# Windowed attention and a 3x3 convolution on one core: one pair of operand stacks instead of two, the work of a unit reordered with a lead per stage, and the row maxima sent through memory

## The reference, cut to what matters

```python
def attention(x):                      # x: (2, 128, 128, 128), already group-normed
    g = clip((x * ac_w + ac_b) * x, 0.0, 6.0)
    q, k, v = windows_and_heads(einsum('bchw,dc->bdhw', g, qkv_w))    # (3, windows, 16, 64, 8)
    attn = softmax(einsum('wnqd,wnkd->wnqk', q, k) * 8 ** -0.5)
    o = einsum('wnqk,wnkd->wnqd', attn, v)
    return einsum('bchw,dc->bdhw', o, proj_w) + proj_b

x = x + attention(group_norm(x))
x = x + conv3x3(group_norm(x), W) + bias
```

## Time and profile before

| | |
|---|---|
| Median of 3 runs | 1791.33 us (1789.05 to 1791.84) |
| Time of the profiled execution | 1795.36 us |
| Its span in the trace | 1793.6 us |
| Busy share of the span: PE, DVE, ACT, POOL | 66%, 55%, 46%, 32% |
| Mean granted clock of TensorE | 0.757 of full |
| DMA, mean over the span | 107 GB/s |

### The profile page before, as it was taken

How to read it: one execution, slowest core, us unless ns; L and a number is a source line. 1 busy time by engine, 2 the same in 40 slices (tenths; PEclk the granted TensorE clock), 3 DMA queues, 4 the chain that set the end, 5 groups by cost and what they waited for, 6 DMA issues and landing times. The chain is left out here.

```text
span 1793.6 us, 62241 instructions
## 1 busy us (share of the span) xinstructions
PE 1177.2 (66%) x25315; PEld 686.1 (38%) x25315; DVE 990.1 (55%) x1379; ACT 824.8 (46%) x1231; POOL 578.0 (32%) x502
## 2 busy tenths in 40 slices
PE   1466666676567767587747665675766667657886
PEld 0244434444344444233314443443444444433332
DVE  7544444444454542699965543544444444418998
ACT  1345545455445553444424554454554555434443
POOL 4122322223222222466521232222231322225665
PEclk8568777777777775699965876776786777658999
DMA  5454544444454550022336453444453544400111
GB/s 207 118 134 126 136 114 115 110 125 125 121 119 114 133 134 22 1 94 100 106 115 161 133 132 103 121 113 107 123 133 97 132 116 127 110 2 12 58 47 71
DMA packets 169202, 191.30 MB, mean 107 GB/s; under 512 B 30208, under 2 KB 145280, under 8 KB 167936
## 3 DMA queue, kind: packets, MB, share of 16 engines
q1 hardware_dynamic: 168960, 187.58, 38.8%
HBM read 118.29 MB, written 67.11 MB: 103 GB/s over the span
## 5 line engine op out<-in xcount | busy, mean ns | idle before, releaser
L485 ACT ACTIVATE work<-ps,ws 128x1024 f32<-128x1024 f32 x256 | 283.9, 1109 | 319.4 <-PE ps L915 317.8
L693 DVE TENSOR_REDUCE m_all<-ps 128x16 f32<-128x1024 f32 x256 | 311.7, 1218 | 133.9 <-PE ps L899 133.7
L940 PE MATMUL ps<-work,v_ext 128*32 128x64 f32 x8192 | 216.1, 261 | 206.5 <-ACT work L485 202.1
L401 POOL TENSOR_TENSOR g_lo<-work,g_hi 128x512 f16<-128x512 f32 x64 | 74.4, 1162 | 673.8 <-ACT g_hi L525 673.8
L940 PEld LDWEIGHTS ps<-work,v_ext 128*32 128x32 f32 x8192 | 166.4, 134 | 248.1 <-issue 125.0
L395 POOL TENSOR_SCALAR work<-work 128x256 f32<-128x256 f32 x128 | 108.5, 848 | 349.5 <-DVE work L687 349.5
L948 PE MATMUL ps<-work,adds 128*32 128x128 f32 x4096 | 210.8, 334 | 0.0
L861 PE MATMUL ps<-work,c_hi 128*128 128x512 f16 x384 | 151.0, 393 | 68.3 <-DVE work L781 68.2
L719 DVE BATCH_NORM_STATS2 st<-img (+1 forms) x64 | 44.4, 694 | 252.7 <-POOL img L408 252.7
L572 ACT CAST work<-work 128x640 f16<-128x640 f32 x128 | 91.7, 718 | 144.4 <-DVE work L777 97.5
L781 DVE TENSOR_TENSOR work<-work 128x640 f16<-128x640 f32 x128 | 152.9, 1197 | 5.0 <-ACT work L572 4.6
(11 more groups left out here) (125 smaller groups left out, 2020.5 us busy)
## 6 DMA issues: line engine op xcount, KB each, us to landing
stack_scratch<-work SPq DMA_DIRECT2D x128, 256.0 KB, 2.2
k_bd<-stack_scratch SPq DMA_DIRECT2D x256, 96.0 KB
q_pl<-stack_scratch SPq DMA_DIRECT2D x128, 192.0 KB, 3.6
q_bd<-stack_scratch SPq DMA_DIRECT2D x256, 96.0 KB
k_pl<-stack_scratch SPq DMA_DIRECT2D x128, 192.0 KB, 4.9
stack_scratch<-work SPq DMA_DIRECT2D x128, 128.0 KB, 2.1
out_dram<-work SPq DMA_DIRECT2D x32, 512.0 KB, 2.7
img<-in_x_dram SPq DMA_DIRECT2D x8, 1024.0 KB, 13.8
```

The costliest lines, as they stand in the source:

```text
L485: a.activation(probs[:, p % 2, :], ps[:, ST_B:ST_B + 2, :].rearrange("p w t -> p (w t)"), ACT.Exp, scale=ws[:, R_EXP:R_EXP + 1]).then_inc( ...
L693: v.tensor_reduce(m_all[:, 0, :, p], ps[:, S_B:S_B + 2, :].rearrange("p r (a k) -> p (r a) k", k=WIN), AX.X, ALU.max).then_inc(max_done, 1)
L940: t_.matmul(ps[32 * k:32 * k + 32, PV_B + p // 2, at:at + WIN], v_pair(md, 2 * p + w, k)[:, 2 * HD * j:2 * HD * j + VC], probs[:, p % 2, c ...
```

## The change

It does five things, all in the attention stage.

1. One pair of stacks. `k_bd` and `q_pl` go. The first scores use `q_bd` and `k_pl` too, now with three buffers each; q is the stationary side, 64 columns at a time, so `scores(p)` is 32 matmuls of 64 columns instead of 16 of 128. Per unit 6 loads of 768 KB in all go.
2. Another order, in which each step names its unit by a lead, from 4 units ahead to 4 behind, and 40 iterations instead of 38. The statistics are taken 4 units late.
3. The hardware loop has 3 iterations in its body and 8 turns, so 7 jumps back for each batch.
4. The affine step is made by VectorE instead of ScalarE.
5. The maxima are written to memory (`max_scratch`, one DMA), and once this has landed two DMAs read them into `q_bd`. The write waits for the loads of the unit before, and the loads and writes of q and k stand behind this wait in SP's queue.

The diff, cut to its core (the reordered calls are those of the lists above, with their waits):

```diff
-TWO = 2
-TURN = 6
+FIRST = 4
...
+    maxd = nc.dram_tensor("max_scratch", [BUFS, PAIRS * HEADS, 2, P], F16, kind="Internal").ap()
...
-        q_pl = sb("q_pl", [P, TWO, HG, UT], F16)
-        k_bd = sb("k_bd", [P, TWO, HG, HJ, UT], F16)
-        k_pl = sb("k_pl", [P, TWO, HG, UT], F16)
-        q_bd = sb("q_bd", [P, TWO, HG, HJ, UT], F16)
+        k_pl = sb("k_pl", [P, BUFS, HG, UT], F16)
+        q_bd = sb("q_bd", [P, BUFS, HG, HJ, UT], F16)
...
+            for i in range(-FIRST, FIRST):
...
+                one(i, i % BUFS, live_at(i))
+            with eng.Fori(0, (UNITS - 2 * FIRST) // BUFS) as t:
+                for k in range(BUFS):
+                    one(t * BUFS + (FIRST + k), (FIRST + k) % BUFS, live_at(FIRST))
+            for i in range(UNITS - FIRST, UNITS + FIRST):
+                one(i, i % BUFS, live_at(i))
...
+                    if live(1):
+                        mb = (m + 1) % BUFS
+                        after(sp, m_hi_done, n + 1)
+                        after(sp, m_lo_done, n + 1)
+                        after(sp, m_in, n)
+                        sp.dma_start(maxd[mb], m_pair[:, :, :]).then_inc(m_sent, 16)
+                        after(sp, m_sent, n + 1)
+                        after(sp, st_done, n + 1 - BUFS)
                         for r in range(HR):
...
+                            at = 64 * r + ROWS
+                            sp.dma_start(q_bd[at:at + 2, mb, :, :, :].rearrange("s g j (p t) -> s (g j) p t", p=PAIRS),
+                                         maxd[mb, 32 * r:32 * r + 32].rearrange("(a p) s t -> s a p t", p=PAIRS)).then_inc(m_in, 16)
+                    if live(3):
+                        after(sp, q_in, n + 2)
+                        after(sp, k_in, n + 2)
+                        write(0, q_lo_done, q_hi_done, q_sent)
+                        write(1, k_lo_done, k_hi_done, k_sent)
+                        after(sp, st_done, n + 3 - BUFS)
+                        after(sp, q_sent, n + 3)
...
+                        after(sp, k_sent, n + 3)
...
+                        after(dve, gpre_done, n + 3)
+                        v.tensor_scalar(aff.rearrange("p (r c) -> p r c", r=WS), img[:, bass.ds(row, WS), bass.ds(col, UCOL)],
+                                        cf[:, A_SLOPE:A_SLOPE + 1], cf[:, A_OFF:A_OFF + 1], ALU.mult, ALU.add).then_inc(aff_done, 1)
...
-                    def scores(p):
-
-                        after(pe, max_done, n + 1, p)
+                    def scores(d, md, p):
+
+                        after(pe, max_done, d, p)
                         settle(pe)
                         for g in range(HG):
...
+                            for j in range(HJ):
+                                for w in range(2):
+                                    tok = slice((2 * p + w) * WIN, (2 * p + w + 1) * WIN)
+                                    at = g * P + j * WIN
+                                    for r in range(HR):
+                                        rows = slice(64 * r, 64 * r + ROWS)
+                                        mm = t_.matmul(ps[64 * w:64 * w + 64, S_B + r, at:at + WIN],
+                                                       q_bd[rows, md, g, j, tok], k_pl[rows, md, g, tok],
+                                                       start=True, stop=True)
```

More of the change, by code:

```diff
@@ L192, in build, with iterations, live_at @@
         block = ctx.enter_context(nc.Block())
[L194 to L202, removed]
-                    late()
[L204 to L209, removed]
+        def iterations(eng, b, one, late=None, at=1 - FIRST):
+            def live_at(i):
+                return lambda lead: 0 <= i + lead < UNITS
+            for i in range(-FIRST, FIRST):
+                if i == at and late:
+                    late()
+                one(i, i % BUFS, live_at(i))
[4 more added lines that the diff above has]
+                one(i, i % BUFS, live_at(i))
         def conv_units(eng, b, one):
@@ L286, in spread @@
                                 at = 64 * r + HROWS * j
[L287 to L291, removed]
-                        for r in range(HR):
[L293 to L315, removed]
+                                sp.dma_start(q_bd[at:at + HROWS, m, :, j, :], q_rows[r, j]).then_inc(q_in, 16)
+                        after(sp, k_sent, n + 3)
+                        k_rows = stackd[m, 1].rearrange("(r g a) s t -> r (a s) g t", r=HR, g=HG)
+                        for r in range(HR):
+                            sp.dma_start(k_pl[64 * r:64 * r + ROWS, m, :, :], k_rows[r]).then_inc(k_in, 16)
                 iterations(sp, b, one)
@@ new lines, in one @@
+                    if live(-4):
+                        row, col = pixels(i - 4)
+                        after(dve, x1_done, n - 4)
+                        v.bn_stats(st[:, bass.ds(i - 4, 1), :].rearrange("p a s -> p (a s)"),
+                                   img[:, bass.ds(row, WS), bass.ds(col, UCOL)]).then_inc(bn_done, 1)
+                    if live(1):
+                        row_max(n + 1, 2)
+                    if live(-1):
+                        scale(n - 1, 1)
+                    if live(1):
+                        row_max(n + 1, 3)
@@ L951, in weigh @@
                         mm.then_inc(pv_done, 1)
-                    def output(d):
-                        after(pe, o_done, d)
-                        t_.matmul(ps[:, GB, :], pw[:, :], o_n, start=True, stop=True).then_inc(proj_done, 1)
-                    me = (m - 1) % TURN
-                    if "B" in on:
-                        after(pe, g_lo_done, n + 2)
-                        after(pe, res_done, n - 3)
-                        if "R" not in on:
-                            after(pe, k_lo_done, n + 1)
-                        if peeled(i, -2) and b:
+                    if live(-1):
+                        weigh(n - 1, (m - 1) % BUFS, 3)
@@ new lines, in one @@
+                    if live(0):
+                        after(pe, m_in, n)
+                        scores_t(n, m, 0)
+                    if live(1):
+                        scores(n + 1, (m + 1) % BUFS, 2)
+                    if live(2):
+                        after(pe, q_lo_done, n + 2)
+                        v_rows()
+                    if live(3):
+                        after(pe, g_lo_done, n + 3)
+                        if live(-2):
+                            after(pe, res_done, n - 2)
+                        else:
+                            after(pe, k_lo_done, n + 2)
+                        if peeled(i, -3) and b:
@@ L1005, in one @@
-                    if "C" in on:
-                        after(pe, scaled_out, n - 1)
-                        after(pe, near_out, n - 1)
+                    if live(0):
+                        scores_t(n, m, 1)
+                    if live(1):
+                        scores(n + 1, (m + 1) % BUFS, 3)
+                    if live(0):
+                        weigh(n, m, 0)
+                    if live(3):
+                        after(pe, v_out, n + 2)
+                        project(0, GA, q_done)
@@ L1008, in one @@
+                    if live(1):
+                        if live(-1):
+                            after(pe, scaled_out, n - 1)
+                            after(pe, near_out, n - 1)
+                        else:
+                            after(pe, m_lo_done, n)
                         after(pe, max_done, n + 1)
```

272 lines of the change are left out of this document (110 added, 162 removed).

## The result

The changed kernel takes 1514.06 us (median of 4 runs, 1509.85 to 1523.93) against 1791.12 for the kernel before (median of 4 runs beside it): a ratio of 0.8463, 95% interval 0.8421 to 0.8504. The prediction was 1490, range 1405 to 1650. Its profiled execution took 1514.4 us, with a span of 1512.7.

A forecast was written before the change was run, and what follows sets the result against it. The prediction took a ring of waits through four engines, 19.48 us per unit, to bound the kernel before. After = 738.6 + 58 T, jumps and clock included; T = 13.0 gives 1493, stated as 1490 us, range 1405 to 1650.

The forecast's parts named there:

- the forecast's case: The prediction's main case for the attention stage: T from 12.4 to 14.5 us, 1490 us in all, chance 0.53.
- T: Predicted period of one unit in the steady attention stage, 13.0 us, where the kernel before has 19.48.
- a ring of waits: Attention stage before: waits through TensorE, ScalarE, GpSimd and VectorE make the 19.48 us period; the change opens it.
- The sum was 11.7 us per unit: TensorE's own attention work per unit at 2.4 GHz: weigh, scores, K, Q, output, V and transposition, 11.7 us.
- The rival of doubled matmuls: The new `scores` takes 0.70 us, twice the old; T = 13.5, 1522 us, chance 0.05.
- The longest is 12.4 ... 13.0 us per unit: Of the rings left in attention, the stacks' is longest at 12.4 us; with 0.6 for hand-offs, 13.0.
- The rings: Waits going round per unit: maxima through memory, 12.2 us, and q and k stacks through SP's queue, 12.4 us.
- 7 x (4.4 + 8.6): Loop jumps back: 7 per batch, each costing 4.4 us in batch 0 and 8.6 in batch 1.
- 21 more for the clock: Low TensorE clock after each of 14 jumps back, 1.5 us each, 21 us.
- Ramp and drain: Start and end of each batch: first two intervals at the old price; up to 10 us gain per batch, counted as nothing.
- The slower rival: The maxima's way through memory takes over the period at a low clock: T 19.4, 1864 us, chance 0.08.
- The rival with one gap and a low clock per unit: Waits gather into one 2 us gap per unit, clock low for some 4.7 us after: T = 15.3, 1626 us, chance 0.22.

The follow-up runs named there:

- The two steps moved by hand: Kernel before with `bn_stats` at the end of VectorE's iteration and ScalarE's second `guesses` ahead of the first exponentials: 1651.06 us, ratio 0.9239.
- the unrolled kernel: The changed kernel with all 40 iterations written out, no loop: 1455.30 us, ratio 0.8145.
- the one without data: The unrolled kernel with the same number of DMAs for q and k but next to no data in them: 1400.45 us, ratio 0.7797.
- the unrolled pair of kernels: The unrolled kernel, 1455.30 us, and the same with each first scores as 16 matmuls of 128 columns, maxima over the wrong side, 1412.29 us.
- three straight-code kernels: The unrolled kernel, 1455.30 us; that without q and k data, 1400.45 us; that with float16 exponentials, v and ones, 1335.74 us.

## Why the prediction was right, and where not

**The total came out, the period did not.** By its own signs the forecast's case would show a period of 14.5 us at most, TensorE busy for about 90% and a clock above 0.9. The 62 intervals are 15.9 us in the mean, and 14.85 to 15.13 in straight code where no jump lengthens them; TensorE is busy for 84%, at 0.89. That the time is still within 24 us of 1490 is luck in part: three errors, worked out below, cancel. (Its sums hold but for a small slip: 1405 us is a T of 11.5, not 11.7.)

**The mechanism held, and the ring had a twin.** The kernel before is bound by a ring of waits, and the new order opens it: the wait at `bn_stats` is down from 252.7 to 10.2 us in the whole run. But the prediction named the one chain, through GpSimd's add and VectorE's 4.11 us. A second one, through ScalarE's exponentials and `guesses`, ended at nearly the same time, and the run with `bn_stats` moved alone gained 1% for it. The forecast did not suffer, since the change moves both. The two steps moved by hand are shown to give 138 us; which parts of the new order give the other half was not taken apart.

**TensorE's own work was priced well.** The sum was 11.7 us per unit. Without "issue" an interval is 11.9 us in the unrolled kernel and, from 14.3 in the same stretch, 11.6 in the one without data; in the changed kernel, at 17.2 in the stretch of its waits, 13.0, part of it at the lower clock. The new `scores` takes 270.45 - 270.08 = 0.37 us, not 0.47: 12 ns for a matmul. So the floor of about 25 ns between starts, in the Trainium skill (TensorE: Matmul & The Clock Gate, "Wait — 56ns, not 53.3ns?"), does not hold for these tiled ones. The rival of doubled matmuls is out for their own time. What they do cost is their share of instructions, 43 us in the unrolled pair of kernels.

**The step that failed is "The longest is 12.4 ... 13.0 us per unit".** It made the rings the bound and left the supply of instructions, 3.2 us per unit in straight code, at nothing. The rings are hidden: the waits for maxima and stacks are 2.2 us in 330. In straight code alone (unrolled) the interval is 14.85 to 15.13. Over the 62 intervals that is 930 us, where the prediction's terms without jumps are 58 x 13.0 + 4 x 19.48 = 832: too little by 98.

**The jumps were priced too high.** The prediction had 7 x (4.4 + 8.6) = 91 us of them in the changed kernel and 21 more for the clock, 112. Taking the loop away gave 59. This is 53 us too much, and the two errors together are 45 of the 47 us by which the 62 intervals (988 us) lie above the forecast for them (1243.9 - 58 x 6.48 + 52 + 21 = 941). The last 2 are batch 1's intervals before, 19.39 us without its jumps where the sum has 19.48. Within the price of a jump the clock was set too low, not too high. The sum took 1.5 us from 4.7 us at the low clock; behind the six jumps between 150 and 450 us TensorE stood for 3.3 to 3.9 us, and the granted clock was then 0.50 for 8 to 9.5 us. That this comes to 4.2 us net is argued, not shown: the unrolled kernel has stops of its own in their place.

**Ramp and drain** were counted as nothing with up to 10 us per batch possible. They gave 10.9 and 15.1, less 1.3 at the start: 25 us. Therefore 1493 + 47 - 25 = 1515, and the profiled execution is at 1514.4. The total was within 2% because 98 too little stands against 53 and 25 too much.

**The maxima and the loads.** From the write's issue at 266.92 to the first read's at 268.93 are 2.0 us, in SP's timeline of the changed kernel, not 2.35:

```profile
266.92 0.46 SPq L276 DMA_DIRECT2D max_scratch<-m_pair  x1
268.93 0.60 SPq L281 DMA_DIRECT2D q_bd<-max_scratch  x2
```

The write lands after 1.8 us (3.2 at most in 64), k's loads after 3.6 instead of the 4.9 of the earlier trace rows. The slower rival needed a way that TensorE waits for in every unit; it waited 1.7 us in 330. The affine step costs nothing, as said. That the six loads less give nothing is not shown: the two pairs of stacks were not tried in the new order, and the run without data, 55 us faster, speaks for some gain from fewer bytes.

**The clock** is at 0.89 in the steady stretch. The rival with one gap and a low clock per unit did not come; such a gap and such a clock came behind those six jumps.

Left open: how the gain beyond the two moved steps divides among the parts of the change; why 6 iterations in the loop's body bring nothing; what, beside their number and the data traffic, makes a packet of instructions late; and whether the way through memory is 1% better than four small DMAs, or the sets differ.

The experiments give a version that beats both kernels without any change of the arithmetic: the changed kernel without its loop, 1455 us. Rounding the second product's operands to float16 as well makes it 1336.

## What to carry to other kernels

Where many small matmuls follow each other without waits, count instructions as well as columns: "issue" time in the middle of a group, at equal distances, points to a supply that comes late, and it can take the place of a wait that is shortened. Before a chain of waits is called the bound, look for another that ends at the same time; moving a single step is a cheap test, and here two moved steps gave half of what a large change did. A jump back of a loop had a net cost of some 4 us for a TensorE kept full; unrolling gave 59 and 60 us in two kernels.

## What the runs showed of the hardware that was not expected

TensorE in this kernel, when it is otherwise kept full, stops for 1 to 2 us at distances of about 124 matmuls with their weight loads, 248 instructions, or of twice that. The distance is about the content of a 16 KB instruction packet, 248 to 254 by the counts of three straight-code kernels. Behind a jump of the loop TensorE stood for 3.3 to 3.9 us in batch 0, and its clock was at 0.50 for 8 to 9.5 us. A group of 32 tiled matmuls of 64 columns takes 0.37 us. With the data traffic cut from 112 to 21 GB/s most of the stops remain, 2.7 of 3.2 us per unit.
